# Both row normalisations of a tile on GpSimd, behind its power, in an attention and feed-forward kernel

## What is computed

```
x = x + attn(layernorm(x))      # differential attention, 16 heads of 2 x 16 dims, 8 KV heads, causal
x = x + ffn(layernorm(x))       # ternary weights 512 -> 2048 -> 512, exact gelu

def layernorm(x, eps=1e-05):
    m = mean(x, -1); v = var(x, -1)
    return (x - m) / sqrt(v + eps)

probs = softmax(rope(q) * scaling @ rope(k).T + causal)       # two maps per head
diff  = probs[:, :, 0] - lambda_full * probs[:, :, 1]
attn  = rmsnorm(diff @ v) * subln_weight * (1 - LAMBDA_INIT) @ Wo.T
ffn   = gelu(h @ w1_q.T + b1) @ w2_q.T + b2
```

## Time and profile before

| | us |
|---|---|
| median of 3 runs | 4375.46 (4370.62 to 4382.93) |
| the profiled execution | 4370.7 |
| its span, first to last instruction | 4368.9 |
| TensorE busy | 3625.1 (83%) |
| VectorE busy | 3369.0 (77%) |
| ScalarE busy | 2913.5 (67%) |
| GpSimd busy | 1495.9 (34%) |
| mean granted TensorE clock | 0.900 |

### The profile page before, as it was taken

One profiled execution on the slowest core, in us unless ns is written; L12 is line 12 of the kernel. 1 busy time (PEld: TensorE's weight loads), 2 busy tenths in 40 slices (PEclk: granted clock), 3 DMA queues, 4 the chain that ended last, 5 costly groups with the idle time before them and its releaser, 6 DMA issues.

```text
span 4368.9 us, 81035 instructions
## 1 busy us (share of the span) xinstructions
PE 3625.1 (83%) x23454; PEld 2157.1 (49%) x23454; DVE 3369.0 (77%) x6188; ACT 2913.5 (67%) x6786; POOL 1495.9 (34%) x1563
## 2 busy tenths in 40 slices
PE   2688888888888888888888988888888888888886
PEld 1345554455445454554545545555545555554553
DVE  6778967888678886788767887678877788678881
ACT  1567766777567775677756766667666777567772
POOL 0243234332333334332343324433134432333323
PEclk7788999989899899998889988999989989899998
DMA  4212112211122112212122110222122111222110
GB/s 133 54 25 41 24 43 43 40 23 33 35 43 43 23 38 46 43 25 38 26 43 43 36 31 23 47 37 43 25 44 43 32 31 25 44 43 43 20 37 14
DMA packets 146768, 166.71 MB, mean 38 GB/s; under 512 B 16640, under 2 KB 117632, under 8 KB 145792
## 3 DMA queue, kind: packets, MB, share of 16 engines
q1 hardware_dynamic: 146304, 161.13, 18.3%
HBM read 105.95 MB, written 55.12 MB: 37 GB/s over the span
## 4 chain that ended last, share of the span: by engine, by line
PE 41%; DVE 25%; issue 19%; ACT 8%; DMA 3%; SPq 2%; POOL 1%; DVEq 1%; ACTq 1%; POOLq 0%
DVE NM L667 9%; PE M L822 7%; PE M L872 7%; PE SP_ L837 6%; PE F L894 6%; PE DP L849 5%; PE F L907 4%; DVE E L691 3%; ACT E L543 3%; DVE CC L688 2%; DMA KST<-scratch 2%; PE M L816 2%; DVE NM L675 2%; PE SP_ L838 1%; PE DX L849 1%
## 5 line engine op out<-in xcount | busy, mean ns | idle before, releaser
L543 ACT ACTIVATE E<-SP_,NM 128x256 f32<-128x256 f32 (+7 forms) x2048 | 1518.3, 743 | 674.7 <-DVE NM L667 461.8
L667 DVE TENSOR_REDUCE NM<-SP_ 128x1 f32<-128x896 f32 (+3 forms) x1024 | 1034.2, 1018 | 257.8 <-PE SP_ L838 254.0
L837 PE MATMUL SP_<-KST,QST 96*128 96x512 bf16 (+3 forms) x3072 | 866.2, 356 | 394.5 <-ACT E L543 329.5
L691 DVE SCALAR_TENSOR_TENSOR E<-E,CC 128x512 f32<-128x512 f32 (+7 forms) x1024 | 928.6, 907 | 36.2
L555 ACT ACTIVATE DT<-DP 128x512 f32<-128x512 f32 (+3 forms) x1024 | 527.7, 515 | 534.9 <-PE DP L849 501.5
L849 PE MATMUL DP<-ident,E 128*128 128x128 f32 x3328 | 617.5, 304 | 140.4 <-DVE E L691 136.7
L675 DVE TENSOR_REDUCE NM<-SP_ 128x2 f32<-128x1024 f32 (+3 forms) x512 | 420.2, 821 | 309.2 <-PE SP_ L838 306.5
L837 PEld LDWEIGHTS SP_<-KST,QST 96*128 96x128 bf16 x3072 | 278.9, 103 | 745.7 <-ACT E L543 515.0
L894 PE MATMUL F<-X2H,W1Q 128*128 128x256 f16 x2048 | 512.1, 287 | 71.0 <-ACT HP L598 67.0
L849 PEld LDWEIGHTS DP<-ident,E 128*128 128x128 f32 x3328 | 395.6, 154 | 313.9 <-issue 164.3
L822 PE MATMUL M<-WQKV,WT 128*128 128x512 f32 x1040 | 531.7, 608 | 8.8 <-DVE T L650 4.1
(11 more groups left out here) (87 smaller groups left out, 4794.6 us busy)
## 6 DMA issues: line engine op xcount, KB each, us to landing
QST<-scratch SPq DMA_DIRECT2D x390, 128.0 KB, 4.4
scratch<-SPL SPq DMA_DIRECT2D x65, 576.0 KB, 2.8
KST<-scratch SPq DMA_DIRECT2D x390, 64.0 KB, 4.8
X<-in_x SPq DMA_DIRECT2D x66, 256.0 KB, 3.3
out<-SQ SPq DMA_DIRECT2D x64, 256.0 KB, 2.0
KST<-in_w1T SPq DMA_DIRECT2D x1, 4096.0 KB, 19.4
DT<-in_w2T SPq DMA_DIRECT2D x1, 4096.0 KB, 28.8
WQKV<-in_wqT SPq DMA_DIRECT2D x1, 1024.0 KB, 6.9
```

Of the source, the lines that this page charges most:

```text
L543: act.activation(dst, score_out(i, 2 * n + k, w), ACT.Exp, bias=NM[:, (2 * u + k) % 8:(2 * u + k) % 8 + 1], scale=1.0, accum_out=SUM[:, i ...
L667: nc.vector.tensor_reduce(NM[:, m:m + 1], score_out(i, 2 * n + k, P * (i + 1)), AX.X, ALU.max, negate=True).then_inc(max_ready, 1)
L691: nc.vector.scalar_tensor_tensor(out=E1[:, u % 2, 0:w], in0=E2[:, e:e + w], scalar=CC[:, u % 2:u % 2 + 1], in1=E1[:, u % 2, 0:w], op0=ALU. ...
L837: pe.matmul(SP_[:, k[a // 512], 0:n], q, KST[0:ROWS, a // P:(a + n) // P, kk, :], start=True, stop=not last)
```

## The change

`normalise` is moved from VectorE's program to GpSimd's, with the same operation and operands; VectorE keeps the statistics. GpSimd makes it at the same half steps (3 and 29), ahead of the `hidden_split` of that half step, and waits for its own power and for TensorE to be done with the former contents of TOK. Since MV and RST are now read by GpSimd, VectorE's `variance` waits for the normalisation before. The diff, with the prologue's call included:

```diff
@@ GpSimd
+            def normalise(j, src, n, done):
+                hold(pool, ln_rstd[j], n + 1)
+                pool.tensor_scalar(TOK[:, :], src, MV[:, 0:1], RST[:, 0:1], ALU.subtract, ALU.mult).then_inc(done, 1)
+
                         if hs == LN1_STATS:
                             rstd(0, T.nb)
+                        if hs == LN1_ROWS:
+                            hold(pool, m_x2t, T.nf)
+                            normalise(0, X[:, (T.t + 1) % 4, :], T.nb, xn_ready)
...
                         if hs == LN2_STATS:
                             rstd(1, T.nf)
+                        if hs == LN2_ROWS:
+                            hold(pool, m_ant, T.nf + 1)
+                            normalise(1, X1[:, (T.t - 1) % 4, :], T.nf, xn2_ready)
...
             rstd(0, 0)
+            normalise(0, X[:, 0, :], 0, xn_ready)
@@ VectorE
-            def normalise(j, src, n, done):
-                after(dve, ln_rstd[j], n + 1)
-                nc.vector.tensor_scalar(TOK[:, :], src, MV[:, 0:1], RST[:, 0:1], ALU.subtract, ALU.mult).then_inc(done, 1)
-
                             after(dve, x_in[(t + 1) % 2], 16 * (b * (TILES // 2) + (t + 1) // 2) + 16)
+                            after(dve, xn2_ready, nf)
                             variance(0, slot, nb)
-                        if hs == LN1_ROWS:
-                            after(dve, m_x2t, nf)
-                            normalise(0, slot, nb, xn_ready)
...
                             after(dve, x1_ready, nf + 1)
+                            after(dve, xn_ready, nf + 2 if T.attend else nf + 1)
                             variance(1, x1, nf)
-                        if hs == LN2_ROWS:
-                            after(dve, m_ant, nf + 1)
-                            normalise(1, x1, nf, xn2_ready)
...
             variance(0, X[:, 0, :], 0)
-            normalise(0, X[:, 0, :], 0, xn_ready)
```

## The result

| | before | after |
|---|---|---|
| median of 6 runs, us | 4373.04 (4364.03 to 4382.93) | 4489.14 (4482.84 to 4497.00) |
| profiled execution, us | 4370.7 | 4489.9 |
| its span, us | 4368.9 | 4488.1 |
| mean granted TensorE clock | 0.900 | 0.900 |

The account below looks back on a forecast made before the run. No engine is full; a loop of engines with fixed instruction order bounds the kernel. 86 (delay) + 11 (clock) - 10 (VectorE's saving) = 87 us on the profiled 4370.7 gives 4458, said as 4460 (factor 1.019), range 4410 to 4500.

Parts of the forecast that it names:

- The bound and the place: No engine is full, a loop across engines sets the time; GpSimd's order at half steps 26 to 29 decides the case.
- The delay, step by step: Second normalisation, odd blocks: TensorE's transposes wait behind two splits; 4.3 us in tiles 1 and 3, 2.7 in tile 5, sum 86.1.
- tile 7: End of a sequence: no loss; a small one would vanish in TensorE's 3.03 us wait for a DMA.
- TensorE's clock: Low-clock stretch at the odd-block stops: 0.5 us taken for each of 23 places, 11 us; bounds 0.4 less to 1.6 more.
- Rival C: Delay absorbed by half in TensorE's waits behind the place: 43 us less 10, about 4408; chance 0.16.
- VectorE's saving: Second normalisation in tiles 2, 4 and 6, where VectorE has no wait: 24 x 0.54 = 13 us, 10 taken.
- The first normalisation: 64 times, TensorE had spare time there: nothing taken; without cover, bounds of 35 us gain and 36 us loss.
- the cover: VectorE's wait for TensorE behind the first normalisation, 2.66 us idle in tile 4's block, swallows the gain and covers collisions.
- B: Dearer: GpSimd's normalisations hold VectorE's difference back (49 us), or the clock reaches its bound (26 more): 4485 to 4510, chance 0.15.
- D: Faster: VectorE's relief wins if the splits end before the power, about 19 us, 4356; chance 0.05.
- the signs named: Odd-tile TOK waits, some 110 us, none in 7; GpSimd order; instruction 0.6 to 0.7 us; even blocks 0.5 shorter; slow clock later.
- rival A: The delay, clock and saving as summed: 4430 to 4490 us; chance 0.64.

Follow-up runs that it names:

- the place mended: The changed kernel, both normalisations on GpSimd, with the second written right behind its power, ahead of hidden_split k=5 and k=6: 4399.7 us, ratio 1.0061.
- the kernel with 0.62 us: The changed kernel with GpSimd's normalisation written as multiply by 1, add 0 (constants), tile not normalised: 4420.6 us, ratio 1.0116.
- wait for split k=6: The kernel before, nothing moved; in blocks with the first product TensorE waits for hidden_split k=6 before the second norm's transposes: 4408.7 us, ratio 1.0095.
- multiply-add per row: The changed kernel with GpSimd's normalisation written as multiply by RST, add MV (two per-row operands), tile not the normalised one: 4439.1 us, ratio 1.0139.
- second one only: Against the kernel before, only the second normalisation is on GpSimd, at half step 29; the first stays on VectorE: 4488.3 us, ratio 1.0263.
- wait for split k=7: The kernel before, nothing moved; in blocks with the first product TensorE waits for the last hidden_split before the second norm's transposes: 4533.5 us, ratio 1.0364.
- subtract-multiply constants: The changed kernel with constants (subtract 0, multiply by 1) for the per-row operands of GpSimd's normalisation, tile not normalised: 4496.1 us, ratio 1.0282.
- place and form mended: Both normalisations on GpSimd as add minus the mean, multiply by RST, the second right behind its power, against the kernel before: 4382.8 us, ratio 1.0018.

## Why the prediction was right, and where it was not

*The bound and the place*: right. GpSimd's order at half steps 26 to 29, hardly visible in a mean of 34%, decides: with the place mended 26 us are left, with it 117; the delay alone makes up to 158.

*The delay, step by step*: the mechanism is right, the price of GpSimd's instruction was mis-sized. The prediction took 0.62 us, with 1.15 as its upper bound; it is 2.08. The bound failed because the nearest row was chosen by size, type and number of inputs, and the operations, multiply-add there and subtract-multiply here, were held to be no matter. The error is 1.46 us at 23 places, 34 us. It also opens two places that the prediction had at nothing: tile 7 (1.1 us, 8 times), where the wait for a DMA took it in as forecast, and tile 0 (1.1 us, 7 times), where 9 us of lateness behind the transposes were down to 4 a few matmuls on. Measured on TensorE's matmuls behind the places in tiles 1, 3 and 5, the delay was 114 us; in the kernel with 0.62 us it was 77, against the 86 of the sum. The Trainium skill (GPSIMD Engine Reference, Engine selection) calls one-input work on GpSimd roughly line-rate; the 0.62 us of multiply-add, against VectorE's 0.54 for its normalisation, agree, the 2.08 us of subtract-multiply do not.

*TensorE's clock*: taken as a cost of 11 us, bounded below at 0.4 us of gain for each place. This step failed at its lower bound: with short stops the loss was some 30 us under the delay. From the mean granted clock c and the span, the time at the lower level is 2 x (1 - c) x span, as the clock has only its two levels. The profiled executions, with the delay measured as said (twelve matmuls behind the transposes, tiles 1, 3 and 5 summed; slow time from the clock before rounding):

| kernel | delay, us | span over before, us | difference | clock | slow time against before's 878, us |
|---|---|---|---|---|---|
| wait for split k=6 | 69 | 33 | -36 | 0.915 | -127 |
| multiply-add constants | 77 | 51 | -26 | 0.912 | -99 |
| multiply-add per row | 83 | 72 | -12 | 0.908 | -58 |
| the change | 114 | 119 | +5 | 0.900 | +21 |
| second one only | 115 | 124 | +10 | 0.893 | +86 |
| wait for split k=7 | 141 (10 in tile 7) | 155 | +14 | 0.894 | +85 |
| subtract-multiply constants | 112 | 134 | +23 | 0.887 | +143 |

All seven lie within 6 us of one line: the delay, less 5 us, plus 0.21 us for each us of slow time. The executions of one and the same kernel agree: the one with multiply-add constants took 4439.8 us at a clock of 0.906 and 4413.2 at 0.916, and over the 140 executions of this case, each set against its own kernel on its own chip, the time grows by 0.27 us with each us of slow time (correlation 0.73). So slow time costs about a quarter of itself, and that is why the change was not 1.5 times dearer than the kernel with 0.62 us but 2.4 times. No run sets the clock by itself, so that the clock is the cause is read from these rows and from tile 6's stretch, not shown by an experiment of its own. Why a given stop moves the slow stretches to where they hurt less stays open. Rival C (half absorbed) gave nearly the right number for the kernel with 0.62 us, 4408 against 4421, by another way: the waits behind did not shrink by half of the delay (77 of 86 us stood), later blocks ran at a higher clock.

*VectorE's saving*: forecast at 10 us for tiles 2, 4 and 6, measured at nothing. That VectorE had no wait there was rightly read, but "no wait" was taken for "the bound", and ScalarE was just behind: a wait of 0.30 us for it stood where the normalisation had been, and the difference beside GpSimd's took 0.21 more. The first normalisation at nothing: right (5 us), and the cover named for it held even with an instruction three times as long.

*Rivals*: B in its first form (collisions everywhere) is out: moving the first alone cost 5 us, and the difference grew from 0.907 to 0.922 us in the mean. The measured 4489 lies in B's span of 4485 to 4510 all the same, by the dearer instruction, which B did not name. D (faster) is out even with place and form mended. Of the signs named, the order, the waits in odd tiles and their absence of harm in tile 7 were seen; "0.6 to 0.7 us" was not, nor were even blocks shorter by 0.5 us (the eight of tile 2 are 2.7 us shorter in all, those of tile 4 6.4 longer), and TensorE waited 155 us, not 110. The 110 do not follow from the prediction's own steps either: 7 x 5.2 + 8 x 5.35 + 8 x 2.7 is 101. One of its signs of being wrong, an instruction of over 1.2 us on GpSimd, did occur.

In all, the forecast of 87 us was 86 of delay, 11 of clock and 10 of saving. The profiled execution has 114 of delay, about 5 of the rest, clock included, and no saving: 119. That the stated range held in spite of an instruction three times as dear is owed to its width, and that 4489 still lies in rival A's span, by 1 us, is luck.

## What to carry to other kernels
Before work is moved to an engine that is idle on average, read that engine's order at the very place: what stands ahead of the new instruction in its queue, when that starts, and who stands still until it is done. Price the instruction by a row with the same operations in the same order, or run it once; on GpSimd, write x - m as x + (-m). And an engine without waits may have a neighbour that is level with it: taking work from one of two then gains next to nothing, adding to it costs nearly all of it (here 0.46 of 0.54 us at the place).

## What the runs showed of the hardware
- GpSimd, 128x512 float32 to float32, one input: multiply-add with constants 0.62 us, with two per-row operands 0.77 to 0.79, add-multiply per row 0.85 in the mean, subtract-multiply with constants 1.93, per row 2.08 to 2.10. VectorE makes the last in 0.54, undisturbed.
- VectorE's difference of 128x640 took 1.10 us beside GpSimd's normalisation and 0.89 otherwise.
- TensorE's mean granted clock differed with the stops put in: 0.900 before, 0.915 with 87 us of added waiting (loss 37 us), 0.894 with 171 us (loss 158). The price of a stop was not in step with its length.
